# Graph attention on one core: GpSimd weighs one head of every pair in two halves, behind each gather

## What is computed

```python
Q, K, V = (x @ Wq), (x @ Wk), (x @ Wv)              # reshaped to (N, 8, 64)
score = einsum('ehd,ehd->eh', K[src], Q[dst]) / sqrt(64)
score = exp(clip(score, -5.0, 5.0))[..., None]
msg = V[src] * score
h_attn = segment_sum(msg, dst) / (segment_sum(score, dst) + 1e-06)
h = x + h_attn
y = (h - mean(h, 0)) * rsqrt(var(h, 0) + 1e-05) * bn_gamma + bn_beta
out = layernorm(x + y)
```

## Time and profile before

| what | before |
|---|---|
| median of 3 runs | 1913.06 us (1907.57 to 1913.44) |
| profiled execution, its own time | 1908.01 us |
| its span | 1906.1 us |
| TensorE busy | 1861.6 us, 98% |
| VectorE busy | 1697.0 us, 89% |
| ScalarE busy | 1367.5 us, 72% |
| GpSimd busy | 1291.3 us, 68% |
| granted TensorE clock, mean | 0.994 |

### The profile page before, as it was taken

How to read it: one execution, slowest core, us unless ns; L and a number is a source line. 1 busy time by engine, 2 the same in 40 slices (tenths; PEclk the granted TensorE clock), 3 DMA queues, 4 the chain that set the end, 5 groups by cost and what they waited for, 6 DMA issues and landing times.

```text
span 1906.1 us, 41424 instructions
## 1 busy us (share of the span) xinstructions
PE 1861.6 (98%) x7904; PEld 1362.2 (71%) x8014; DVE 1697.0 (89%) x2454; ACT 1367.5 (72%) x4602; POOL 1291.3 (68%) x1473
## 2 busy tenths in 40 slices
PE   7999999998999999999999999999999999999897
PEld 4555555554888888878888888888888888887333
DVE  6677755644999999999999999999999999999888
ACT  0002000002999999999999999999999999998857
POOL 0205666103777888788888888888888888885677
PEclk9999999999999999999999999999999999999999
DMA  5547788546999999999999999999999999999307
GB/s 183 162 151 250 288 319 274 186 161 231 357 358 356 362 367 358 346 351 368 368 356 353 352 366 369 354 355 355 366 361 358 360 355 365 370 358 370 122 33 287
DMA packets 184521, 589.09 MB, mean 309 GB/s; under 512 B 28480, under 2 KB 30240, under 8 KB 184480
## 3 DMA queue, kind: packets, MB, share of 16 engines
q0 software_dynamic: 135904, 465.14, 65.8%
q1 hardware_dynamic: 45120, 121.69, 17.8%
q10 hardware_dynamic: 3456, 1.78, 0.3%
HBM read 535.27 MB, written 78.91 MB: 322 GB/s over the span
## 4 chain that ended last, share of the span: by engine, by line
PE 74%; DVE 16%; issue 4%; DMA 4%; ACT 1%; POOL 1%; SPq 0%; DVEq 0%; ACTq 0%; POOLq 0%
PE acc L939 29%; PE places L342 22%; PE q_ps L923 17%; DVE kv L795 6%; DVE raw L806 5%; DMA kv<-kv_d,idx 2%; PE mm_ps L949 2%; PE banks L1151 1%; DVE stats L1288 1%; DVE agg L1281 1%; PE mm_ps L951 1%; PE places L402 1%; DMA q_tile<-xb_d 1%; POOL kv L751 1%; PE banks L1142 1%
## 5 line engine op out<-in xcount | busy, mean ns | idle before, releaser
L751 POOL DMA_INDIRECT kv<-kv_d,idx x880 | 887.0, 1008 | 339.2 <-issue 204.8
L846 ACT ACTIVATE kv<-kv 128x64 f32<-128x64 f32 x3520 | 889.0, 335 | 14.3
L939 PE MATMUL acc<-kv,mm_sb 128*128 128x260 f32 x3520 | 845.6, 383 | 4.1 <-POOL kv L714 2.2
L939 PEld LDWEIGHTS acc<-kv,mm_sb 128*128 128x128 f32 x3520 | 654.3, 190 | 137.9 <-issue 32.8
L923 PE MATMUL q_ps<-q_tile,mm_sb 128*128 x1760 | 559.2, 439 | 5.6 <-DVE kv L795 4.9
L795 DVE TENSOR_TENSOR kv<-q_ps,kv 128x1024 f32<-128x1024 f32 x440 | 536.1, 1218 | 14.0 <-PE q_ps L923 7.0
L806 DVE TENSOR_REDUCE raw<-kv 128x16 f32<-128x1024 f32 x440 | 532.2, 1210 | 0.0
L923 PEld LDWEIGHTS q_ps<-q_tile,mm_sb 128*128 128x128 f32 x1760 | 328.6, 189 | 74.4 <-DVE kv L795 20.8
L714 DVE TENSOR_TENSOR kv<-kv 128x384 f32<-128x384 f32 (+1 forms) x440 | 271.6, 617 | 0.1
L857 ACT ACTIVATE mm_sb<-mm_ps,less 128x1024 fp32r<-128x1024 f32 x220 | 241.2, 1096 | 13.1 <-remote 10.1
L435 ACT COPY p<-places 128x768 f32<-128x768 f32 x23 | 18.4, 798 | 243.5 <-PE places L342 243.5
(11 more groups left out here) (171 smaller groups left out, 1358.6 us busy)
## 6 DMA issues: line engine op xcount, KB each, us to landing
q_tile<-q_d SPq DMA_DIRECT2D x49, 512.0 KB, 7.2
kv<-kv_d,idx POOLq DMA_INDIRECT x880, 6.2
kv_d<-kv_a SPq DMA_DIRECT2D x25, 512.0 KB, 5.5
xb<-in_x POOLq DMA_DIRECT2D x49, 256.0 KB, 4.3
xb_d<-xb POOLq DMA_DIRECT2D x49, 256.0 KB, 3.7
out_rows<-agg SPq DMA_DIRECT2D x49, 256.0 KB, 2.1
x_sb<-in_xT SPq DMA_DIRECT2D x24, 512.0 KB, 7.9
q_d<-q_a SPq DMA_DIRECT2D x24, 512.0 KB, 4.1
```

The source lines that it names most:

```text
L751: pool.indirect_dma_start(kv[:, s, u, 0:2 * DIM], None, kv_d, bass.IndirectOffsetOnAxis(idx[:, s, u:u + 1], 0), bounds_check=N_NODES - 1, ...
L846: return act.activation(v, v, ACT.Copy, scale=kv[:, s, u, 2 * DIM + h:2 * DIM + h + 1])
L939: last = pe.matmul(acc[:, bass.ds(par, 1), DIM - (1 - n) * HALF:DIM + n * HALF], m, kv[:, sc, u, DIM + n * HALF:DIM + (n + 1) * HALF], sta ...
```

## The change

The function `weigh_visit` is new: it weighs GpSimd's one head of a single visit, 128 x 64. In every step, and no longer in every second one, GpSimd waits for the exponentials of pair p and weighs its first visit between the two gathers of pair q, behind the copy of indices where there is one. Behind the second gather it weighs the second visit, and only this operation raises `s_v`. VectorE weighs three heads in every pair, and TensorE waits for three signals per filling in every pair.

```diff
+        def weigh_visit(eng, s, u):
+
+            first = HEADS - POOL_HEADS
+            v = kv[:, s, u, DIM + first * D_HEAD:2 * DIM]
+            w = kv[:, s, u, 2 * DIM + first:KVW].broadcast_to([P, D_HEAD])
+            return eng.tensor_tensor(v, v, w, ALU.mult)
...
                     gather(q, s, fills, 0)
                 if there(q + 2) and s % IDX_PAIRS == IDX_PAIRS - 2:
                     index(q + 2, *at(s, fills, 2))
+                if there(p):
+                    wait_apart(pool, s_exp[sp], fp)
+                    weigh_visit(pool, sp, 0)
                 if there(q):
                     gather(q, s, fills, 1)
-                if s % 2 and there(p):
-                    wait_apart(pool, s_exp[sp], fp)
-                    weigh(pool, sp, HEADS - POOL_HEADS, POOL_HEADS).then_inc(s_v[sp], 1)
+                if there(p):
+                    weigh_visit(pool, sp, 1).then_inc(s_v[sp], 1)
...
                     dve.wait_ge(s_exp[s2], f2)
-                    weigh(dve, s2, ACT_HEADS, HEADS - ACT_HEADS - (POOL_HEADS if s % 2 == 0 else 0)).then_inc(s_v[s2], 1)
+                    weigh(dve, s2, ACT_HEADS, HEADS - ACT_HEADS - POOL_HEADS).then_inc(s_v[s2], 1)
...
-                    pe.wait_ge(s_v[sc], (2 if sc % 2 else 3) * fc)
+                    pe.wait_ge(s_v[sc], 3 * fc)
```

## The result

The changed kernel takes 2039.36 us, the median of four runs, against 1910.99 us before (a fourth run moved that median from 1913.06): a ratio of 1.0673, 95% interval 1.0649 to 1.0696. That is 128 us more, where 60 were predicted; the direction was right and the size was not. The time lies at the very end of the stated range, 1918 to 2040 us, and above the forecast's own, 1930 to 1995. The upper part of the range was there for case C, which is not what happened, so the result lies inside it by luck.

What follows compares the result with a forecast made beforehand. GpSimd, with less than 0.03 us a pair left, was taken as the bound, TensorE nearly as full. 3.01 + 0.03 + 0.02 + 0.01 = 3.07 us a pair, 0.14 more, times 440 gave +60 us: 1970 us, range 1918 to 2040.

Steps and rivals of the forecast that it cites:

- case C: GpSimd's weighings lock onto VectorE's: 0.20 us a pair added, 2058 us, or 2014 at 0.1 us; chance 0.14.
- Step 3: Between gathers: each 0.30 us gap becomes 0.45 us with a small weighing; GpSimd needs 3.01 us a pair.
- Step 2: GpSimd's new 128 x 64 weighing: 0.27 us each, with bounds of 0.204 and 0.30 us.
- Step 4: GpSimd's weighings meeting VectorE's: the usual pair should escape; 0.03 us a pair taken for disturbed stretches.
- Steps 1, 5 and 6: VectorE's relief, at best 0.03 us a pair; GpSimd's earlier wait for exponentials, 0.02; TensorE's third signal, nothing by itself.
- A: GpSimd's small operation is cheap, under 0.22 us with collisions; TensorE's 2.90 us decides: 1895 to 1900 us; chance 0.10.
- B: A draw: GpSimd lands on 2.93 us a pair again, 1908 to 1918 us; chance 0.08.
- D: GpSimd's wait for the exponential becomes the bound, needing 0.85 us of lateness in ordinary pairs; no chance given apart.

Runs made afterwards that it cites:

- f2_reduce: The changed kernel with VectorE's weighing replaced by a sum over the same columns, reading one tensor: 1975.99 us, ratio 1.0354.
- g3_two_heads: The changed kernel, but VectorE weighs heads 4 and 5 only, head 6 left unweighed: 1988.33 us, ratio 1.0419.
- h1_pad_ahead: The changed kernel with an added VectorE sum over 96 columns ahead of its weighing in every pair: 1983.91 us, ratio 1.0395.
- g4_half_head: The changed kernel, but each GpSimd operation weighs 128 x 32, half of head 7 left unweighed: 1943.15 us, ratio 1.0186.
- g1_together: The changed kernel, but one GpSimd operation of 128 x 128 behind the second gather weighs both visits in every pair: 1946.56 us, ratio 1.0207.
- h2_pad_behind: The changed kernel with an added VectorE sum over 96 columns behind its weighing in every pair: 1986.68 us, ratio 1.0414.
- f3_nopool: The changed kernel, but GpSimd weighs only the last five pairs, VectorE weighs four heads in all others: 1915.31 us, ratio 1.0033.

## Why the prediction was right or wrong

**The bound: right.** GpSimd had 0.02 us a pair left before, and with one weighing behind every gather it sets the pace. The sums of its operations and the pairs as measured, in us:

| kernel | gather | weighing | sum per pair | pair |
|---|---|---|---|---|
| the change | 1.103 | 0.302 | 3.21 | 3.23 |
| f2_reduce | 1.029 | 0.300 | 3.06 | 3.08 |
| g3_two_heads | 1.046 | 0.303 | 3.10 | 3.12 |
| h1_pad_ahead | 1.031 | 0.308 | 3.08 | 3.10 |
| g4_half_head | 1.031 | 0.253 | 2.97 | 3.01 |
| g1_together | 1.018 | 0.476 | 3.01 | 3.02 |

Each sum is two gathers, the weighings, 0.18 us for each weighing's gaps, 0.04 for the copy (g1_together: one weighing, 0.30 for the plain gap and 0.02 for the copy).

**Step 3, the gaps: right.** 0.02 us ahead of a weighing and 0.16 behind it stayed, and the copy cost 0.15 rather than 0.21 us: the weighing behind it starts 0.15 us after it (1002.99 and 1003.14 above).

**Step 2, the size of the small operation: too small.** 0.302 us for the 0.27 taken, at the bound that the copy and the 0.41 gave. The line from 512 columns has the wrong slope down here: 128 columns 0.41, 64 columns 0.302, 32 columns 0.253 us give 1.6 ns a column and 0.20 fixed. That is 0.06 us a pair, less 0.015 for the cheaper copy: about 0.05 us, 22 us in all.

**Step 4, contention: the term that failed.** I had "There a gather runs" and "So the usual pair should escape", and took 0.03 us a pair. The case was priced only for the weighings on GpSimd (rival C); a gather that begins inside VectorE's weighing had no price, although the trace of the kernel before held its price: 21 gathers that begin so, at 1.16 us in place of 1.0. In the change it is 0.15 us a pair, 52 us more than taken. The place in time was right for the pair that I had assumed and not for the one that came. VectorE's weighing does start 5.0 us behind the end of a second weighing of GpSimd (1001.82 to 1006.81 above) where the mask products lie between, and mostly 4.6 to 4.8 us behind it where they do not, much as the expectation of h1_pad_ahead says. With a pair of 3.0 us, 5.0 is 2.0 us into the next, behind the second gather's start at 1.66, as in g4_half_head and h1_pad_ahead, where the median is 2.15. In the changed kernel the median is 1.63, since a caught gather makes its own pair longer and so brings VectorE's next weighing forward: the place is that 5.0 or 4.7 us less the length of the pair before. The trace shows a cycle of one round of eight pairs (medians of each slot, 600 to 1700 us; all in us, places from the end of the last second weighing):

| slot | behind the second weighing two pairs back | pair before | place of VectorE's weighing | second gather starts | caught | pair |
|---|---|---|---|---|---|---|
| 6 | 4.78 | 3.02 | 1.76 | 1.80 | 25 of 43 | 3.55 |
| 7 | 5.01 | 3.55 | 1.47 | 1.67 | 27 of 43 | 3.24 |
| 0 | 4.70 | 3.24 | 1.47 | 1.67 | 39 of 43 | 3.24 |
| 1 | 5.03 | 3.24 | 1.79 | 1.67 | 11 of 43 | 3.02 |
| 2 | 4.61 | 3.02 | 1.59 | 1.80 | 30 of 42 | 3.39 |
| 3 | 5.00 | 3.39 | 1.60 | 1.67 | 41 of 42 | 3.38 |
| 4 | 5.06 | 3.38 | 1.68 | 1.67 | 2 of 42 | 3.02 |
| 5 | 5.01 | 3.02 | 1.98 | 1.67 | 2 of 42 | 3.02 |

So a meeting brings the next one or misses it narrowly: the second gathers of slots 1, 4 and 5 escape because VectorE starts behind them, in slot 4 within 0.03 us of them, and that of slot 6 is caught only because the copy puts it 0.13 us later. The eight lengths give 3.23 us in the mean, the pair as measured. That the place decides is what g4_half_head, h1_pad_ahead and h2_pad_behind show; why slot 4 comes at 5.06 and not at 4.7 us, and what sets a round on this cycle, is open. The two errors together, 22 + 52, take the predicted 60 to 134 us; the profiled execution lost 132. So the mechanism that was forecast, GpSimd as the bound, is right, and the term for meetings was put at 0.03 us a pair where the runs show 0.15.

**Steps 1, 5 and 6** were small, as predicted: ahead of its weighings GpSimd waited 9.0 us for exponentials in the whole span, and of the three signals that TensorE now waits for in every pair, GpSimd's is the one that the profile names. What VectorE gained, 0.13 us in every second pair, is part of the 124 us in which it stands idle.

**The rule of the Trainium skill**, page "SBUF — State Buffer", section "Who interferes with whom", says that a VectorE instruction with two SBUF inputs contends with GpSimd instructions that read SBUF, but of an earlier probe that `tensor_copy` stalled DMA while `tensor_tensor` and `tensor_reduce` did not. The runs agree for the reduce (1.029 us) and differ for the two-input multiplication: 1.29 us in the mean for a gather that begins inside it, and 1.02 for one that had begun before (1000.47 above). The measurement decides.

**Rivals.** A and B would have needed a small operation under 0.23 us. C named the right pair of engines and the wrong operation: GpSimd's small weighings, at 0.302 us, are as long as in f2_reduce, where VectorE's weighing is replaced by a sum (0.300). D did not occur.

## What to carry to other kernels

Before work goes to an engine that issues gathers, add up its operations with the fixed gaps between them; an engine that the page gave 68% busy was full in this stage. Price a meeting with the other engines for every kind of instruction on that engine, the gathers too, and work out the place in time for each kind of round. Once such an engine sets the pace, a small difference can tip nearly all pairs into or out of a meeting (0.10 us a pair did it in g4_half_head), so compare a single operation against two halves and try the operation in another gap.

## What the runs showed of the hardware that I had not expected

- A gather issued by GpSimd that begins during a VectorE multiplication of two SBUF tensors is held: 0.94 us + 0.84 of the rest of that multiplication, from 0.15 us to go (f3_nopool). One that began 0.12 us earlier is not (1.02 us), and neither were 21 that began within the multiplication's first 0.03 us (1.02 to 1.03 us). During a sum of one tensor it is not either (1.04 us).
- Added work made a kernel faster: 0.24 us a pair on VectorE took the ratio from 1.070 to 1.040, with VectorE's weighing behind the second gather's start and no longer ahead of it.
- The same kernel before took 1908 us on one chip and 2110 us on another, and three kernels with ratios of 1.003 to 1.035 on the one lay within 0.4% of it on the other.
